# A graph layer with a running segment maximum: the order of TensorE's step is changed

## The reference, cut to what matters

```python
def ref(x, edge_index, W1, b1, W2, b2):        # N = 12500 nodes, E = 400000 edges, 64 channels
    x_i = x[dst]; x_j = x[src]                  # dst is sorted
    feat = concatenate([x_i, x_j - x_i], axis=-1)
    h = maximum(feat @ W1 + b1, 0.0) @ W2 + b2
    out = segment_max(h, dst, num_segments=N)
    return where(isneginf(out), 0.0, out)

h = maximum(layernorm(x), 0.0)
x = x + ref(h, stack([src, dst]), W1, b1, W2, b2)
```

## Time and profile before

| | |
|---|---|
| median of 3 runs | 5022.33 us (5005.23 to 5023.61) |
| the profiled execution | 5046.15 us, span 5044.3 us |
| mean granted TensorE clock | 0.794 |
| matmuls / weight loads of TensorE | 3240.3 / 1876.2 us |
| VectorE, ScalarE, GpSimd busy | 2493.6 / 1025.4 / 3109.6 us |

### The profile page before, as it was taken

How to read it: one execution, slowest core, us unless ns; L and a number is a source line. 1 busy time by engine, 2 the same in 40 slices (tenths; PEclk the granted TensorE clock), 3 DMA queues, 4 the chain that set the end, 5 groups by cost and what they waited for, 6 DMA issues and landing times.

```text
span 5044.3 us, 58734 instructions
## 1 busy us (share of the span) xinstructions
PE 3240.3 (64%) x14598; PEld 1876.2 (37%) x14861; DVE 2493.6 (49%) x8363; ACT 1025.4 (20%) x4057; POOL 3109.6 (62%) x3186
## 2 busy tenths in 40 slices
PE   2100137777777777777777777777777777777970
PEld 2100014444444444444444444444444444444540
DVE  4100115555555555555555555555555555556871
ACT  4300212212122121221212222122221212212320
POOL 5777756666666666666666666666666666664017
PEclk8555558888888888888888888888888888888985
DMA  7866312222222222222222222222222222222222
GB/s 274 315 229 227 115 32 73 67 73 70 70 73 67 73 70 70 70 70 73 70 70 69 70 73 69 70 70 69 73 67 73 70 70 72 69 72 71 80 77 56
DMA packets 239614, 452.86 MB, mean 90 GB/s; under 512 B 94781, under 2 KB 95402, under 8 KB 238738
## 3 DMA queue, kind: packets, MB, share of 16 engines
q1 hardware_dynamic: 97663, 225.75, 14.2%
q0 software_dynamic: 103216, 117.29, 11.1%
q10 hardware_dynamic: 38362, 105.62, 5.4%
HBM read 230.84 MB, written 217.71 MB: 89 GB/s over the span
## 4 chain that ended last, share of the span: by engine, by line
another core or an unknown queue 41%; issue 28%; DVE 10%; ACT 9%; PE 7%; POOL 2%; ACTq 2%; DMA 1%; DVEq 1%; POOLq 0%; SPq 0%
ACT dst_all L549 5%; DVE state L911 4%; PE ps_g L676 4%; DVE a_fill L885 3%; PE ps_m L696 2%; POOL a_rows L456 2%; ACT zt L560 2%; ACTq L567 1%; DMA shared<-in_x_dram 1%; DVE rows L897 1%; ACT zt L474 1%; ACT keep L531 1%; PE ps_t L687 0%; ACT shared L501 0%
## 5 line engine op out<-in xcount | busy, mean ns | idle before, releaser
L393 POOL DMA_INDIRECT rows<-b_table,src_idx x2865 | 2785.5, 972 | 1523.6 <-issue 805.7
L676 PE MATMUL ps_g<-shared,dst_all 128*128 128x512 bf16 x9468 | 2318.6, 400 | 174.3 <-issue 170.5
L676 PEld LDWEIGHTS ps_g<-shared,dst_all 128*128 128x128 bf16 x9731 | 1011.1, 105 | 1329.5 <-issue 417.3
L696 PE MATMUL ps_m<-w_diag,zt 128*128 128x128 f32 x3126 | 707.8, 411 | 920.2 <-ACT zt L560 917.8
L696 PEld LDWEIGHTS ps_m<-w_diag,zt 128*128 128x128 f32 x3126 | 638.2, 308 | 1056.3 <-ACT zt L560 1049.8
L911 DVE SCALAR_TENSOR_TENSOR state<-state,keep,ps_m 128x64 f32<-128x64 f32 x3125 | 862.3, 276 | 202.5 <-PE ps_m L696 166.7
L885 DVE SCALAR_TENSOR_TENSOR a_fill<-a_fill,keep 128x64 f32<-128x64 f32 x3144 | 879.6, 280 | 53.1 <-DVE a_fill L885 41.6
L935 DVE TENSOR_TENSOR dst_all<-ps_s,page_keys 128x1664 bf16<-128x1664 f32 x132 | 249.6, 1891 | 816.0 <-remote 795.1
L935 DVE TENSOR_TENSOR dst_all<-ps_x,page_keys 128x1664 bf16<-128x1664 f32 x132 | 249.6, 1891 | 794.7 <-remote 774.7
L560 ACT ACTIVATE zt<-ps_t 128x512 f32<-128x512 f32 (+1 forms) x521 | 226.4, 486 | 1517.9 <-remote 1511.6
L549 ACT ACTIVATE dst_all<-ps_g,dst_all 128x64 f32<-128x64 f32 x2096 | 458.1, 347 | 33.2 <-DVE rows L944 33.2
(11 more groups left out here) (116 smaller groups left out, 877.0 us busy)
## 6 DMA issues: line engine op xcount, KB each, us to landing
a_edges<-state SPq DMA_DIRECT2D x80, 1250.0 KB
a_fill<-a_edges SPq DMA_DIRECT2D x260, 384.0 KB
states<-state ACTq DMA_DIRECT2D x260, 384.0 KB
rows<-b_table,src_idx POOLq DMA_INDIRECT x2865
src_idx<-in_src_dram SPq DMA_DIRECT2D x234, 6.0 KB
shared<-in_x_dram SPq DMA_DIRECT2D x5, 625.0 KB
b_table<-shared ACTq DMA_DIRECT2D x5, 625.0 KB
a_table<-a_rows SPq DMA_DIRECT2D x1, 3125.0 KB
```

The costliest lines, as they stand in the source:

```text
L393: nc.gpsimd.indirect_dma_start(out=rows[:, slot, t * C:(t + 1) * C], out_offset=None, in_=b_table, in_offset=at(src_idx[:, slot, :], t)).t ...
L676: last = nc.tensor.matmul(ps_g[:, half, :], key_is[:, half, g, :], table[:, g, t, :], start=(g, t) == (0, 0), stop=g == PAGES - 1)
L696: last = nc.tensor.matmul(ps_m[:, g, a * C:(a + m) * C], zt[0:m * C, g, a * C:a * C + P], w2_pair[0:m * C, 0:m * C], start=True, stop=True)
```

## The change

TensorE's step becomes: messages of c, transposes of c+1, keys of c+5, all 13 pages of the pick of c+3 in one run. The transposes of chunk 0 stand ahead of the loop. Before the messages of a group TensorE now also waits for the maxima of the group before in the same PSUM bank; for that `max_step` starts higher by one chunk. ScalarE's step begins with the relu of c, and flags and keys follow it.

```diff
@@ ScalarE
             def step(c, k, tiles=CHUNK):
-                if tiles == CHUNK:
-                    flags(c + FILL_AHEAD, k + FILL_AHEAD)
-                    spread_keys(c + KEYS_AHEAD, k + KEYS_AHEAD)
                 for g, n in groups(tiles):
                     act.wait_ge(z_turned, c * GROUPS + g + 1)
...
                 if tiles == CHUNK:
+                    flags(c + FILL_AHEAD, k + FILL_AHEAD)
+                    spread_keys(c + KEYS_AHEAD, k + KEYS_AHEAD)
                     mask(c + CHOOSE_AHEAD, k + CHOOSE_AHEAD)
-                act.wait_ge(max_step, c * CHUNK + tiles + 1)
+                act.wait_ge(max_step, (c + 1) * CHUNK + tiles + 1)
@@ TensorE
-            def pick(c, k, pages):
+            def pick(c, k):
                 half = k % 2
-                if pages[0] == 0:
-                    pe.wait_ge(keys_matched, c + 1 + FREE)
-                    pe.wait_ge(octet_masked, c - 1 + FREE)
-                for g in pages:
+                pe.wait_ge(keys_matched, c + 1 + FREE)
+                pe.wait_ge(octet_masked, c - 1 + FREE)
+                for g in range(PAGES):
...
-            def step(c, k, tiles=CHUNK):
-                whole = tiles == CHUNK
-                for g, n in groups(tiles):
+            def turn(c, k):
+
+                for g, n in groups(CHUNK):
                     pe.wait_ge(z_ready, c * GROUPS + g + 1)
...
-                if whole:
-                    pick(c + PICK_AHEAD, k + PICK_AHEAD, range(PAGES_FIRST))
+            def make_messages(c, tiles=CHUNK):
+
                 for g, n in groups(tiles):
                     pe.wait_ge(relu_done, c * GROUPS + g + 1)
+                    pe.wait_ge(max_step, c * CHUNK + g * GROUP + n + 1)
...
-                if whole:
-                    turn_keys(c + KEYS_AHEAD, k + KEYS_AHEAD)
-                    pick(c + PICK_AHEAD, k + PICK_AHEAD, range(PAGES_FIRST, PAGES))
+            def step(c, k):
+                make_messages(c)
+                turn(c + 1, (k + 1) % RING)
+                turn_keys(c + KEYS_AHEAD, k + KEYS_AHEAD)
+                pick(c + PICK_AHEAD, k + PICK_AHEAD)
...
+            turn(0, 0)
             with pe.Fori(0, ITERS) as i:
                 for k in range(RING):
                     step(i * RING + k, k)
-            step(CHUNKS, 0, TAIL)
+            make_messages(CHUNKS, TAIL)
@@ VectorE
-            dve.sem_inc(max_step, 1)
+            dve.sem_inc(max_step, CHUNK + 1)
...
-                dve.wait_ge(max_step, c * CHUNK + t + 1)
+                dve.wait_ge(max_step, (c + 1) * CHUNK + t + 1)
```

More of the change, by code:

```diff
@@ L62, in edge_conv @@
     FILL_AHEAD = 3
-    PAGES_FIRST = PAGES // 2 + 1
     with ExitStack() as ctx:
@@ L677, in pick @@
                                                 start=(g, t) == (0, 0), stop=g == PAGES - 1)
-                if pages[-1] == PAGES - 1:
-                    last.then_inc(picked, 1)
-            def step(c, k, tiles=CHUNK):
-                whole = tiles == CHUNK
-                for g, n in groups(tiles):
+                last.then_inc(picked, 1)
+            def turn(c, k):
+                for g, n in groups(CHUNK):
                     pe.wait_ge(z_ready, c * GROUPS + g + 1)
@@ L709, in _ @@
                 if c >= -PICK_AHEAD:
-                    pick(c + PICK_AHEAD, c + PICK_AHEAD, range(PAGES))
+                    pick(c + PICK_AHEAD, c + PICK_AHEAD)
+            turn(0, 0)
             with pe.Fori(0, ITERS) as i:
@@ L713, in _ @@
                     step(i * RING + k, k)
-            step(CHUNKS, 0, TAIL)
-            pe.wait_ge(max_step, CHUNKS * CHUNK + TAIL + 1)
+            make_messages(CHUNKS, TAIL)
+            pe.wait_ge(max_step, (CHUNKS + 1) * CHUNK + TAIL + 1)
             nc.tensor.transpose(ps_s[0:C, P:2 * P], state[:, 0, (TAIL - 1) * C:TAIL * C], ident[:, :]).then_inc(last_turned, 1)
```

## The result

The changed kernel took 5103.52 us (median of 4 runs, 5100.98 to 5107.27), the kernel before 5019.24 us beside it (4 runs, 5005.23 to 5023.61). The ratio is 1.0173, 95% interval 1.0152 to 1.0195: the change costs 1.7%. The forecast was no change; the time lies on the slower side of it.

The account below looks back on a forecast made before the run. Gather steps were taken as bound by a loop of TensorE's held signal and eleven gathers (16.6 us), the last 26 by TensorE. All terms summed to 0 us, so 5022 us; own range 4997 to 5047, wide range 4700 to 5130.

Parts of the forecast that it names:

- What bounds a gather step: Gather stage: a loop of transposes' signal, eleven gathers (13.84 us) and the wait for the held signal, together 16.6 us.
- The last 26 steps: Steps without gathers: TensorE's sum stays about 10.03 us each; 0 us taken, bounds 0 to 13 us.
- The chain's place in the step: Gather stage: match, maxima, relu, messages, transposes end at T+12.0 to T+14.1, leaving 2.5 to 4.6 us slack; 0 us.
- T: Moment in a gather step when the transposes' signal arrives, 2500.1 in the rows; first gather at T+0.84.
- Is the signal still held?: Gather stage: transposes would be TensorE instruction 60 to 94 of the train, beyond the held one (58); still held, 0 us.
- Rival 1: GpSimd freed early, trains lose pauses: 4739 us if every second goes, 4456 if all; chance 0.32, of which 0.12 below 4700.
- Rival 2: Longer chain becomes the bound, GpSimd idles for late transposes: up to 5700 to 6100 us; chance 0.23 with mild forms.
- mild form: Rival 2 with the longer chain costing only 0.4 us per step: 5115 us.
- Pages in one run: TensorE's two halves of pages become one; spacing stays 0.216 us, nothing is late: 0 us.
- ScalarE's order: Relu first, flags and key spread (1.1 us) behind it; key matmul and mask still covered: 0 us.
- the added wait: TensorE's wait for maxima of c-1 before messages of c, always met because relu queues behind them: 0 us.
- all pauses go: Rival 1's extreme, by the skill page's rule: 566 us saved, 4456 us, and down to some 260 us less.

Follow-up runs that it names:

- b_narrow: Kernel before with 36 of its 37 page matmuls per chunk 128 columns wide instead of 512; 5020.88 us (one run), kernel before 5039.06.
- a_plain: Changed kernel unaltered, on a chip that does not hold signals; 4089.15 us against 4084.9 for the kernel before, ratio 1.0013.
- a_pause_5: Changed kernel, GpSimd also waiting until its gathers of the chunk before have landed, chip holding signals; 4982.89 us (one run), kernel before 5014.09.
- a_onepart: Changed kernel with 13 page matmuls per chunk instead of 37; 4936.06 us (one run), kernel before 5039.06.

## Why the prediction was wrong, point by point

- **What bounds a gather step: right.** "Signal, 0.8 us, eleven gathers, about 1.9 us until the held signal" is the step of all 234 trains before and of 144 after (16.62 and 16.56 us). b_narrow shows that TensorE's busy time is no part of it.
- **The last 26 steps: right.** Messages at 4743.36 and 4753.39 in TensorE's timeline, 10.03 us, transposes and 37 pages between. The 9 us more behind the last gather lie inside the bound of 13 us that I gave; where they come from is open.

```profile
4743.36 1.50 PE L693 MATMUL ps_m<-w_diag,zt 128*128 128x128 f32 x12
4744.70 0.82 PE L683 MATMUL ps_t<-ident,rows 128*128 128x128 f32 x6
4745.41 8.15 PE L673 MATMUL ps_g<-shared,dst_all 128*128 128x512 bf16 x37
4753.39 1.50 PE L693 MATMUL ps_m<-w_diag,zt 128*128 128x128 f32 x12
```

- **The chain's place in the step: wrong.** I put relu at T + 9.5 and the end of the transposes at T + 12.0 to T + 14.1, behind a whole chain from match to maxima. With T 0.8 us ahead of the first gather, the transposes ended at T + 4.8 (2504.59) and T + 5.2 (2521.37) in the rows shown. Over all trains they ended 4.4 us after the first gather in the double ones and 9.5 us in the single ones (medians), so about T + 5.2 and T + 10.3. The relu does wait for the maxima, as I had it (148 times in the list of waits), but the phase of the chain against the train is not fixed: in many steps it moved to the front of the train. This alone cost nothing (16.56 us in single trains), but it fed the next step.
- **"Is the signal still held?": this step failed.** I computed the transposes as number 60 to 94, with 12 to 29 pages ahead of them, and took "held" for every step. They were number 44 to 104, so with 4 to 34 pages ahead of them; 5 and 8 in the rows shown. The border that I estimated at 30 to 50 lies at about 50 in this kernel, so the idea and even its size held. What was wrong is the count and, with it, one answer for 234 steps: 90 chunks went in double trains, 144 did not. The order of before is safe at 66, since keys and pages stand between its messages and the next transposes.
- **Rival 1: mechanism right, sign wrong.** Double trains did come, as it said, and the trace shows its mark (22 gathers without the 2.77 us idle). But it priced a double train at 14.19 + 16.61 = 30.80 us, 2.42 us saved each; measured are 34.48 us. It did name the reason, that without a pause the pages' signals are held for two trains, but gave it no price. The rows for that were at hand: during gathers TensorE gets one instruction per transfer. A step has 112 instructions (56 matmuls). Some 50 to 60 run ahead, the rest crawls, so a second train in a row can't be fed. The term left out is TensorE's starvation: idle behind a double train 6.88 us, where rival 1 left the 2.77 us of a single one.
- **Rival 2: the mark was seen, not its mechanism.** GpSimd idles over 3 us behind fresh transposes, 39 times from 1000 to 4500 us, and the kernel is slower by 84 us where its mild form gave 93. But relu and messages were not late because the chain had grown: the single trains of the same kernel have the same chain and take 16.56 us, a_plain has it and loses 0.1%, and a_pause_5 has it and loses nothing.
- **Pages in one run, ScalarE's order, the added wait: 0 us, not contradicted.** Only ScalarE's order was tried alone, and only on chips that do not hold signals: with the old order the changed kernel takes 1.0035 and 1.0036 of the kernel before, with the new one 1.0013 on another chip, so relu first may be worth 0.2% there. Pages in one run and the added wait were never taken back alone.
- **The page of the Trainium skill.** On the chips where the kernel before takes 5012 to 5039 us, the runs go against what "PSUM — Partial Sum Buffer", section "Engine vs sequencer instructions", states, that an update attached to an engine's instruction fires when it completes, by the number above (relu 11.6 us after its transposes). On those with 4077 to 4085 us nothing is seen that goes against it: between the gathers of a_plain's loop no gap is longer than 0.32 us, and rival 1's "all pauses go" is the kernel that runs there (4456 us and up to 260 less in its pricing, 4089 measured), before the change as well as after.

## What to carry to other kernels

A producer's pause may be what lets the consumer work. Before costing a freed engine at its gain, ask what the others can do while it runs on; here TensorE gets one or two instructions per transfer. A rule of counting ("number 58 is held") must be applied to the spread of a step's phases, not to one step: with 44 to 104 around a border at 50, some steps go the other way. And a result that hangs on such a border can differ from chip to chip: the same change costs 1.7% on one sort and 0.1% on the other.

## What the runs showed of the hardware

- **Two sorts of chips.** The kernel before takes 5039 and 5013 us on two chips, and 4077, 4078, 4077 and 4085 us on four others. The case's own runs (5019 us) are of the first sort; the record does not say whether their chip is a third one. The gathers' own pace is the same (1.25 us a start). The difference is when TensorE's signals arrive beside gathers. What sets the sort is open: nothing in the traces names it.
- **Signals of about 50 TensorE instructions are prompt in a train** (46 to 48 out, 50 to 52 not, in the rows shown), counted in instructions and not in TensorE's busy time (b_narrow). This is worked out from the counts; no row shows a signal leaving. It is no sharp rule: in the kernel after a few double trains have their transposes at up to 62, and a_onepart has single trains at 36 where the transposes come late in the train. What is counted, and from where, is open.
- **One or two TensorE instructions per transfer afterwards**: a matmul with its load each 2.1 to 2.8 us in the double train shown and each 1.4 us in b_narrow, beside gathers each 1.25 us. What sets the pace between these is open. TensorE gets about 46 to 56 instructions past the last prompt signal before it starves, an estimate from two trains that takes 50 prompt signals and one more per gather: in the train of 2517.00 number 2 x (5 + 12 + 6 + 1 + 34) = 116 at 12.0 us, when ten gathers had started (116 - 50 - 10 = 56), and in that of 2500.63 number 104 to 106 at 9.9 us, when eight had (46 to 48). The Trainium skill, "TensorE: Matmul & The Clock Gate", its opening table, gives TensorE's queue a depth of 64; the estimate is near that, and whether it is this queue that fills was not tried.
- **Other engines' signals.** In the kernel after ScalarE waits 3.31 us for "remote" ahead of L536 at 2533.97, whose input VectorE had written at 2529.65, in the kernel before VectorE 1.10 us between two maxima: in such trains more than TensorE's signals is late. How far this adds to the price of a double train is open.
